# Values of an attention chunk multiplied three chunks behind their scores instead of four, and the normalising chain one chunk sooner

## The chip, the cores and the metric

The kernel runs on one core of one Trainium2 chip. The metric is the device time of one execution in microseconds (us). Three executions of the kernel before took 1441.52, 1445.03 and 1444.88 us, a median of 1444.88 us. Engines go by the profile's names: PE is TensorE (PEld its loading of weights), DVE is VectorE, ACT is ScalarE, POOL is GpSimd, SP is SyncE.

## The reference

The input x is 4 batches of 1024 tokens of width 128. After a layer norm, two branches are added to x: causal attention with 16 heads of width 64, and a mixture of 8 experts of which each token takes two. The change touches the attention alone:

```python
sim = einsum('bhid,bhjd->bhij', q, k)            # q scaled by 64 ** -0.5
attn = softmax(where(causal_mask, -max, sim))
out = einsum('bhij,bhjd->bhid', attn, v)
return out.reshape(b, n, h * d) @ w_out
```

## The kernel before, in words

The first stage (up to about 260 us) does the experts and lays the normalised tokens out. The second stage is the attention, and all of this case lies there. It goes through 64 heads (4 batches x 16 heads), two heads of one batch after each other (a pair shares a projection and half of `w_out`), and eight heads, numbered 0 to 7 here, make a group: one pair of heads over the four batches. Eight groups follow each other.

A head's score matrix is worked off in twelve chunks (`chunks`, L1026), one to each step 0 to 11. A chunk is 128 keys against up to 512 queries; its widths in order are 512, 128, 384, 256 for the first half of the queries, then 512, 128, 512, 256, 512, 384, 512, 512 for the second. The narrower ones lie on the diagonal.

One list, `order`, written out by `beside` (L1064 to L1105), sets the program of every engine: each engine walks through the same list and does its own part of each entry, in order. A step `c` of head `g` enters, in this sequence: the scores of chunk `c` ("score"); the values of the chunk `LAG` steps back ("pv"); one part of the next head's row maxima ("max", in steps 0, 1, 2, 3, 5, 7, 10, 11, L1039); the low part of those values ("pv_low"); in even heads a projection of the next pair ("project", steps 1, 2, 3, 5, 6, 10) with its subtraction ("project_lo"); an output projection ("y", step 11 of even heads and step 10 of odd ones); the transposed maxima ("shift", steps 8 and 0); the entries of `CHAIN`; and a piece of the experts' combination ("gather" in heads 1 and 2, "combine" in heads 3 to 7).

What the entries are on the engines:

- score (L1484): PE multiplies keys by queries (L1497, L1498, and L1500 for a mask). ACT takes the exponential twice (L1281), once to `probs` and once rounded to `p_hi`; POOL subtracts the two to `p_lo` (L1243). There are two score banks, four `probs` and six `p_hi` and `p_lo`.
- pv and pv_low (L1503, L1519): PE multiplies `p_hi` by the values twice (L1514, L1516) and waits for `p_split` before it multiplies `p_lo` (L1525). After the last chunk of a half, ACT copies the sums out to `raw` (L1297), at the place of that "pv_low" in the list.
- max (L1457): PE makes raw scores in `max_ps` (L1472, L1475), and DVE reduces them (`maximum`, L1322, the reduction on L1329). There are two banks; a narrow part takes one and a wide part (the last four) both. PE waits on L1466 until the part named in `BEFORE` (L1043) is reduced; the part of step 5 is wide and so waits for that of step 3.
- project: ACT copies PE's product out (L1259, L1263), DVE subtracts it from the product (L1319, L1307).
- the chain, for each half: SP folds the row sums (L1154), DVE inverts them (L1378), SP stores the inverse to DRAM (L1160) and spreads it back over 64 partitions (L1166), DVE multiplies `raw` by it ("normalise", `heads`, L1384). `LAST` says that a half ends with chunk 3 or 11, and `CHAIN` says how many steps after the scores of that chunk each entry stands.
- combine: DVE's small operations on `x_row` and `gvar` (L1342 to L1372), fed by POOL's gathers of rows (L1236, eight in each group, in steps 7 to 11 of head 1 and 1, 3, 5 of head 2).

The wait between the scores and their low values is this one, with `n_chunk(g, c)` counting chunks:

```python
pe.wait_ge(p_split, n_chunk(g, c) + 1)
pe.matmul(head_ps[0:HEAD + 1, cols], v_hi[i][:, j, s], p_lo[:, slot, 0:width], ...)
```

Of the kernel before, what the change touches and what calls it, by code (L numbers as in the profile page):

```python
# [24 lines left out]
def attention_and_experts(nc, x, attn_gamma, w_qkv, w_out, w_router, b_router,  # L25
# [28 lines left out]
    with ExitStack() as whole:  # L54
# [925 lines left out]
        with ExitStack() as ph2:  # L980
# [48 lines left out]
            CH = len(chunks)  # L1029
            DIAG = [q0 == j * P for _, j, q0 in chunks]  # L1030
            WIDTH = [(half + 1) * BANK - q0 for half, _, q0 in chunks]
            LAG = 4
            CHAIN = [("fold", 5), ("invert", 8), ("store", 9), ("spread", 12), ("normalise", 16)]
            G = BATCH * 2
            ALL_HEADS = PAIRS * G
            ALL_PAIRS = PAIRS * BATCH
# [27 lines left out]
            def beside(at):  # L1064
# [9 lines left out]
                if g == 0 and c in FIRST_WIDE:  # L1074
                    order += [("max", 0, m) for m in FIRST_WIDE[c]]
                values = at >= LAG and (at - LAG) // CH < ALL_HEADS
                if values:
                    order.append(("pv", (at - LAG) // CH, (at - LAG) % CH))
                max_at = MAX_AT if g else FIRST_MAX_AT
                if g + 1 < ALL_HEADS and c in max_at:  # L1080
                    order.append(("max", g + 1, max_at.index(c)))
                if values:
                    order.append(("pv_low", (at - LAG) // CH, (at - LAG) % CH))

# [9 lines left out]
                if g < ALL_HEADS and c == (0 if g else 2):  # L1094
                    order.append(("shift", g, 1))
                for kind, lag in CHAIN:
                    if at >= lag and (at - lag) // CH < ALL_HEADS and (at - lag) % CH in LAST:
# [483 lines left out]
```

## Time and profile before

| | |
|---|---|
| median of three executions | 1444.88 us |
| the profiled execution | 1440.34 us, of which its span is 1438.6 us |
| second stage | from about 260 us to the end |
| PE busy | 1360.5 us, 95% of the span |
| DVE, ACT, POOL busy | 1102.6, 1046.0 and 940.8 us |
| mean granted TensorE clock | 0.983 of full speed |

The span is the time from the first to the last instruction on the core, and the profiled execution's own time is 1.7 us longer than it. Busy shares are averages over the whole span: PE's idle time lies mostly in the first stage, and in the second stage each wait has to be looked up where it stands. A row of a timeline gives the start from the beginning of the span, the length, the engine and line, the operation with its output and inputs, and in brackets how long the engine was idle before and for whom. Several instructions of one kind in a row are merged (x2, x3). Lengths of neighbours overlap somewhat, so that what one costs in a row of its kind is the spacing of their starts.

### The profile page before, as it was taken

How to read it: one execution, taken by the hardware profiler on the slowest of the kernel's cores; microseconds unless marked ns; L12 is line 12 of the kernel's file. 1: busy time of each engine (PE TensorE's matmuls, PEld its weight loads, DVE VectorE, ACT ScalarE, POOL GpSimd, SP SyncE). 2: the span in 40 equal slices, each digit the busy share in tenths (PEclk: the TensorE clock that was granted, in tenths of full speed). 3: DMA queues.
4: the chain of work that ended last, by engine and by line, in shares of the span. 5: the costliest groups of instructions: out<-in, count | busy, mean ns of one | idle time of the engine just before them, and what ended most of it. 6: DMA issues, size and time to landing. Idle time of an engine off the chain costs nothing.

```text
span 1438.6 us, 26847 instructions
## 1 busy us (share of the span) xinstructions
PE 1360.5 (95%) x8618; PEld 1017.9 (71%) x8618; DVE 1102.6 (77%) x1944; ACT 1046.0 (73%) x2571; POOL 940.8 (65%) x933
## 2 busy tenths in 40 slices
PE   2789999899999999999999999999999999999996
PEld 2778999566777676767677767677767676767674
DVE  5756666569877987798869886988698869886974
ACT  1556666587877777778777877787877787778774
POOL 1676000387668766876687668766876687668775
PEclk9789999899999999999999999999999999999998
DMA  9132231121212121212121212121212122212212
GB/s 337 42 102 83 62 92 52 45 64 46 51 46 69 45 52 42 70 43 51 40 71 43 50 40 69 45 51 40 70 44 51 42 67 48 51 46 65 49 46 78
DMA packets 80377, 89.87 MB, mean 62 GB/s; under 512 B 17736, under 2 KB 58992, under 8 KB 80240
## 3 DMA queue, kind: packets, MB, share of 16 engines
q1 hardware_dynamic: 59168, 69.90, 19.2%
q10 hardware_dynamic: 16976, 9.86, 2.2%
q0 software_dynamic: 4096, 8.40, 2.0%
q8 instruction: 72, 1.18, 0.3%
q14 instruction: 65, 0.53, 0.1%
HBM read 37.25 MB, written 16.78 MB: 38 GB/s over the span
## 4 chain that ended last, share of the span: by engine, by line
PE 55%; DVE 21%; POOL 3%; issue 2%; ACT 1%; DMA 1%; POOLq 0%; ACTq 0%
PE max_ps L1472 8%; PE score_ps L1497 7%; PE score_ps L1498 7%; PE head_ps L1525 7%; DVE row_max L1329 7%; PE head_ps L1514 6%; PE head_ps L1516 6%; PE misc_ps L1535 3%; DVE x_row L1342 3%; DVE q_a L1319 3%; PE misc_ps L1453 2%; DVE k_b L1319 2%; POOL p_lo L1243 2%; PE max_ps L1475 2%; DVE heads L1384 2%; PE score_ps L1500 2%
## 5 line engine op out<-in xcount | busy, mean ns | idle before, releaser
L1243 POOL TENSOR_TENSOR p_lo<-probs,p_hi 128x512 fp32r<-128x512 f32 (+3 forms) x768 | 797.2, 1057 | 291.1 <-ACT p_hi L1281 288.1
L1281 ACT ACTIVATE probs<-score_ps 128x512 f32<-128x512 f32 (+3 forms) x768 | 376.7, 491 | 180.9 <-PE score_ps L1500 100.0
L1329 DVE TENSOR_REDUCE row_max<-max_ps 128x1 f32<-128x1024 f32 x508 | 383.5, 756 | 153.0 <-PE max_ps L1475 148.8
L1281 ACT ACTIVATE p_hi<-score_ps 128x512 fp32r<-128x512 f32 (+3 forms) x768 | 376.6, 490 | 0.0
L1497 PE MATMUL score_ps<-q_a,k_a 128*128 128x512 f32 (+3 forms) x768 | 287.2, 374 | 2.4 <-ACTq L1250 1.5
L1525 PE MATMUL head_ps<-p_lo,v_hi 128*65 128x512 f32 (+3 forms) x768 | 276.1, 360 | 1.1 <-POOL p_lo L1243 1.1
L1514 PE MATMUL head_ps<-p_hi,v_hi 128*65 128x512 f32 (+3 forms) x768 | 274.8, 358 | 0.0
L1498 PE MATMUL score_ps<-q_b,k_b 65*128 65x512 f32 (+3 forms) x768 | 267.0, 348 | 0.0
L1516 PE MATMUL head_ps<-p_hi,v_lo 128*64 128x512 f32 (+3 forms) x768 | 258.3, 336 | 0.0
L1472 PE MATMUL max_ps<-k_a,q_a 128*128 128x512 f32 x764 | 230.6, 356 | 19.8 <-DVE row_max L1329 18.9
L1472 PEld LDWEIGHTS max_ps<-k_a,q_a 128*128 128x128 f32 x764 | 130.2, 190 | 71.5 <-DVE row_max L1329 43.5
L1497 PEld LDWEIGHTS score_ps<-q_a,k_a 128*128 128x128 f32 x768 | 146.2, 190 | 37.8 <-ACT p_hi L1281 5.9
L1498 PEld LDWEIGHTS score_ps<-q_b,k_b 65*128 65x128 f32 x768 | 146.2, 190 | 10.0
L1525 PEld LDWEIGHTS head_ps<-p_lo,v_hi 128*65 128x65 f32 x768 | 110.4, 144 | 22.6 <-POOL p_lo L1243 8.4
L1516 PEld LDWEIGHTS head_ps<-p_hi,v_lo 128*64 128x64 f32 x768 | 105.8, 138 | 25.0
L1514 PEld LDWEIGHTS head_ps<-p_hi,v_hi 128*65 128x65 f32 x768 | 111.6, 145 | 11.5
L1384 DVE TENSOR_TENSOR heads<-raw,scale 64x512 f32<-64x512 f32 x128 | 116.3, 909 | 3.0 <-DMA scale<-inv_rows 1.1
L1500 PE MATMUL score_ps<-later,ident 128*128 128x128 bf16 x512 | 118.6, 232 | 0.0
L1475 PE MATMUL max_ps<-ident,later 128*128 128x128 bf16 x508 | 117.3, 231 | 0.0
L1319 DVE TENSOR_TENSOR q_a<-misc_ps,q_a 64x512 fp32r<-64x512 f32 x124 | 85.5, 690 | 36.0 <-ACT q_a L1259 33.2
L1475 PEld LDWEIGHTS max_ps<-ident,later 128*128 128x128 bf16 x508 | 49.0, 96 | 88.5 <-issue 72.8
L553 ACT ACTIVATE w_raw<-bank,b1T 128x128 f32<-128x128 f32 x312 | 88.9, 368 | 24.9 <-PE bank L907 24.3
(190 smaller groups left out, 2171.5 us busy)
## 6 DMA issues: line engine op xcount, KB each, us to landing
k_a<-k_a SPq DMA_DIRECT2D x64, 256.0 KB, 4.0
q_b<-q_a SPq DMA_DIRECT2D x64, 256.0 KB, 4.2
scale<-inv_rows SPq DMA_DIRECT2D x128, 128.0 KB, 2.8
sorted_x<-zeros SPq DMA_DIRECT2D x13, 384.0 KB, 11.6
sorted_y<-result ACTq DMA_DIRECT2D x78, 64.0 KB
w_raw<-sorted_x SPq DMA_DIRECT2D x25, 192.0 KB, 2.4
acc<-in_L_attn_x_dram SPq DMA_DIRECT2D x4, 512.0 KB, 8.1
w_raw<-in_L_ffn_W_dram ACTq DMA_DIRECT2D x4, 512.0 KB, 12.7
```

Of the source, the lines that this page charges most:

```text
L1243: pool.tensor_tensor(p_lo[:, slot, 0:w], probs[:, n_chunk(g, c) % PROBS, 0:w], p_hi[:, slot, 0:w].bitcast(F32), ALU.subtract).then_inc(p_s ...
L1281: ins = act.activation(p[:, n_chunk(g, c) % ring, 0:width], score_ps[n_chunk(g, c) % 2][:, 0:width], ACT.Exp, scale=SCALE)
L1319: ins = dve.tensor_tensor(lo, src[s * HEAD:(s + 1) * HEAD, :], hi, ALU.subtract)
L1329: dve.tensor_reduce(row_max[:, g % 2, t:t + 1], src, axes, ALU.max).then_inc(max_taken, 1)
L1472: ins = pe.matmul(max_ps[:, b, 0:w], rows, k_a[i][s][:, k0:k0 + w], start=True, stop=not last)
L1475: ins = pe.matmul(max_ps[:, b, w - P:w], later[:], ident16[:], start=False, stop=True)
L1497: pe.matmul(dst, k_a[i][s][:, keys], q_a[i][s][:, qs], start=True, stop=False)
L1498: ins = pe.matmul(dst, k_b[i][s][:, keys], q_b[i][s][:, qs], start=False, stop=not DIAG[c])
L1500: ins = pe.matmul(dst[:, 0:P], ident16[:], later[:], start=False, stop=True)
L1514: pe.matmul(head_ps[0:HEAD + 1, cols], v_hi[i][:, j, s], p_hi[:, slot, 0:width], start=(j == 0), stop=False)
L1516: pe.matmul(head_ps[0:HEAD, cols], v_lo[i][:, j, s], p_hi[:, slot, 0:width], start=False, stop=False)
L1525: pe.matmul(head_ps[0:HEAD + 1, cols], v_hi[i][:, j, s], p_lo[:, slot, 0:width], start=False, stop=c in LAST).then_inc(pv_done, 1)
```

## The change

The values follow their scores three steps later instead of four, and each of the five entries of the chain stands one step sooner: the fold 4 steps after the scores instead of 5, the inverse 7 instead of 8, the store 8 instead of 9, the spread 11 instead of 12, the normalising 15 instead of 16. Since the values also come one step sooner, each entry keeps its distance to the values. Banks, rings and every other entry of the list stay where they are.

```diff
-            LAG = 4
-            CHAIN = [("fold", 5), ("invert", 8), ("store", 9), ("spread", 12), ("normalise", 16)]
+            LAG = 3
+            CHAIN = [("fold", 4), ("invert", 7), ("store", 8), ("spread", 11), ("normalise", 15)]
```

In step numbers: the copy to `raw` moves from steps 7 and 3 to 6 and 2, the fold from 8 and 4 to 7 and 3, the inverse from 11 and 7 to 10 and 6, the store from 0 and 8 to 11 and 7, the spread from 3 and 11 to 2 and 10, the normalising from 7 and 3 to 6 and 2 (first half, second half; all of a later head than the scores, except for the first half's copy, fold and inverse).

## Rows read from the trace of the kernel before

**Rows 1.** The page: busy time by engine, share of the span, instructions.
```profile
PE 1360.5 (95%) x8618; PEld 1017.9 (71%) x8618; DVE 1102.6 (77%) x1944; ACT 1046.0 (73%) x2571; POOL 940.8 (65%) x933
```

**Rows 2.** Waits, whole span: who waited for whom, us in total, times, longest us.
```profile
PEld max_ps L1472 <- DVE row_max L1329: 43.5, 85, 1.7
...
PE max_ps L1472 <- DVE row_max L1329: 18.9, 28, 1.4
...
PEld head_ps L1525 <- POOL p_lo L1243: 8.4, 18, 1.2
```

**Rows 3.** Timeline of ACT, steps 2 and 3 of head 0 of group 4.
```profile
708.90 1.21 ACT L1259 ACTIVATE q_a<-misc_ps 64x512 fp32r<-64x512 f32 x2
...
710.68 0.59 ACT L1297 ACTIVATE raw<-head_ps 65x512 f32<-65x512 f32 x1
711.15 1.21 ACT L1259 ACTIVATE k_a<-misc_ps 64x512 fp32r<-64x512 f32 x2
```

**Rows 4.** Timeline of DVE, same head: work entered in steps 2 to 5.
```profile
709.52 1.39 DVE L1319 TENSOR_TENSOR q_a<-misc_ps,q_a 64x512 fp32r<-64x512 f32 x2
710.95 0.69 DVE L1329 TENSOR_REDUCE row_max<-max_ps 128x1 f32<-128x512 f32 x1
711.78 1.39 DVE L1319 TENSOR_TENSOR k_b<-misc_ps,k_a 64x512 fp32r<-64x512 f32 x2
713.09 0.68 DVE L1384 TENSOR_TENSOR heads<-raw,scale 64x512 f32<-64x512 f32 x1
713.79 1.23 DVE L1329 TENSOR_REDUCE row_max<-max_ps 128x1 f32<-128x1024 f32 x1
```

**Rows 5.** Timeline of POOL, same head, step 3.
```profile
710.87 0.74 POOL L1243 TENSOR_TENSOR p_lo<-probs,p_hi 128x256 fp32r<-128x256 f32 x1 [0.84 <-ACT p_hi L1281]
```

**Rows 6.** Timeline of PE, same head: scores of step 4, of step 5, wide maxima.
```profile
710.69 0.40 PE L1497 MATMUL score_ps<-q_a,k_a 128*128 128x512 f32 x1
...
711.87 0.22 PE L1497 MATMUL score_ps<-q_a,k_a 128*128 128x128 f32 x1
...
712.23 0.68 PE L1472 MATMUL max_ps<-k_a,q_a 128*128 128x512 f32 x2
```

**Rows 7.** Timeline of POOL, heads 1 and 2 of group 4: first gather, and after the last.
```profile
734.73 1.24 POOL L1236 DMA_INDIRECT two_y<-sorted_y,places  x1
...
754.52 5.92 POOL L1243 TENSOR_TENSOR p_lo<-probs,p_hi 128x512 fp32r<-128x512 f32 x5
```

**Rows 8.** Timeline of PE, head 2: low values of chunk 5 and of chunk 6.
```profile
753.95 0.22 PE L1525 MATMUL head_ps<-p_lo,v_hi 128*65 128x128 f32 x1
...
755.87 0.47 PE L1525 MATMUL head_ps<-p_lo,v_hi 128*65 128x512 f32 x1
```

**Rows 9.** Timeline of DVE, end of head 2 and start of head 3.
```profile
754.48 1.92 DVE L1384 TENSOR_TENSOR heads<-raw,scale 64x512 f32<-64x512 f32 x1
...
760.70 2.31 DVE L1342 TENSOR_SCALAR x_row<-x_row,mean,rstd 128x128 f32<-128x128 f32 x1
```

**Rows 10.** Timeline of PE: step 7 of head 3, step 11 of head 6.
```profile
768.68 0.68 PE L1472 MATMUL max_ps<-k_a,q_a 128*128 128x448 f32 x2 [0.47 <-DVE row_max L1329]
...
831.80 0.55 PE L1472 MATMUL max_ps<-k_a,q_a 128*128 128x320 f32 x2 [1.38 <-DVE row_max L1329]
```

**Rows 11.** Timeline of DVE, head 4: the chain's operations right behind step 7's maxima.
```profile
791.62 0.33 DVE L1378 RECIPROCAL inv<-den 16x32 f32<-16x32 f32 x1
791.98 0.88 DVE L1384 TENSOR_TENSOR heads<-raw,scale 64x512 f32<-64x512 f32 x1
```

**Rows 12.** Timeline of PE, head 4: maxima of step 7 and of step 10.
```profile
788.48 0.67 PE L1472 MATMUL max_ps<-k_a,q_a 128*128 128x448 f32 x2 [0.22 <-DVE row_max L1329]
...
792.13 0.51 PE L1472 MATMUL max_ps<-k_a,q_a 128*128 128x384 f32 x2
```

**Rows 13.** The chain that ended last, its longest stretch on POOL, last head.
```profile
1409.73 12.61 POOL p_lo L1243 x11
```

**Rows 14.** The page: DMA issues, KB each, us to landing.
```profile
scale<-inv_rows SPq DMA_DIRECT2D x128, 128.0 KB, 2.8
```

## The prediction

> **What bounds the kernel now.** I read the page first: PE is busy for 95% of the span [rows 1], so in the second stage time is gained or lost by what makes PE wait, and by nothing else. The view of waits says for what: PE and its weight loads wait 62 us at most for DVE's row maxima (43.5 and 18.9, partly the same time) and 8.4 us for POOL's low parts, in 18 places [rows 2]. The low values are the wait that the change tightens, since PE asks for them a whole step sooner; the maxima are a wait that it touches indirectly, since it reorders DVE. So I went to the timelines of both, in the heads where little is in hand.
>
> Of 768 low values that is few, and they lie together, once in each group. From head 1's step 7 on, eight gathers of about 1 us stand between POOL's subtractions, and POOL works through from 734.73 to 760.44 [rows 7]. At 755.87 PE starts the low values of chunk 6 the moment POOL delivers them [rows 8]: there even four steps are only just enough. For DVE, head 0 of a group shows what it does in steps 2 to 5 of every even head [rows 4]: after ACT's copy it subtracts a projection (709.52), reduces the maxima of step 3 (710.95), subtracts the next projection, normalises (713.09) and reduces the wide maxima of step 5 (713.79). PE asked for those wide maxima's banks at 712.23 [rows 6]; step 3's were reduced at 711.64, 0.59 before.
>
> **The change part by part.** *Work.* No instruction is added or removed, on any engine. The values run one set ahead of where they were against the scores; over all chunks PE does the same.
>
> *ACT's copy to raw, from step 3 to 2 in even heads.* It now stands ahead of the copies of the projection that DVE waits for. It costs ACT 0.47 (711.15 - 710.68) [rows 3], so those copies start at 709.37 instead of 708.90, and DVE's pair at 709.99 instead of 709.52; the pair takes 1.43 to the next start [rows 4], to 711.42. POOL's subtraction in step 3 moves as much, from 710.87 to 711.34, and ends at 712.08 [rows 5].
>
> *The normalising of the second half, from step 3 to 2.* Before, it stood behind the maxima of step 3 on DVE; now it stands in front of them. That is the edit's dearest effect. Alone it costs 0.70 (713.79 - 713.09) [rows 4]. At 711.42, though, POOL's subtraction has just begun, and both read SBUF. Such meetings are in the trace: the normalising at 754.48, beside a POOL subtraction that starts at 754.52, took 1.92 instead of 0.68 [rows 4, 7, 9]. So it ends at 712.1 at the least and at about 712.7 if it waits, and the maxima of step 3, 0.69 long, are reduced at 712.8 or 713.4. I take the second, because in the nearest row DVE lost even by starting 0.04 sooner.
>
> *What PE asks in step 5.* Step 4 took 1.18 with five 512-wide matmuls, 0.236 each; the five narrow ones before the wide maxima in step 5 took 0.36, 0.07 each [rows 6]. Now step 4's three value matmuls are 128 wide (-0.49) and step 5's first two 384 wide (+0.21): PE asks at 712.23 - 0.28 = 711.95. It waits until 713.4: **1.45 us** per even head (0.87 if normalising does not wait). Behind that wait on PE stand the low values and the third projection of the step, and ACT and DVE wait for the latter. In odd heads there is no projection, DVE idles before these maxima, and I put the same edit at nothing; without that cover it costs up to 0.15 in 24 heads.
>
> *The low values in heads 1 and 2.* POOL's stretch is fixed by its own queue while it is behind. The low values of chunk 6 now stand a step sooner, right where those of chunk 5 stood at 753.95, and POOL is ready at 755.87: 1.92 late. About 0.4 of this the kernel before already pays in the steps around. So 1.5 per group. It falls into the same steps as the 1.45 of head 2 and mostly hides it: I take 1.7, between 1.4 (one hides the other) and 2.9 (both in full).
>
> *Head 3.* DVE's first operation there lasts 2.31, waiting out POOL's backlog [rows 9], and so PE waits in step 7 (0.47 and the weight load before it) [rows 10]. Once PE is late by 1.7 the backlog is gone sooner: 0.6 back, between 0 and 1.1.
>
> *Head 4.* Reciprocal and normalising of the first half move from behind the maxima of step 7 to in front, 1.24 (792.86 - 791.62) [rows 11]. Those maxima were ready at 791.6, and PE asked at 792.13 [rows 12]. DVE is besides 0.6 late (1.4 later, less the 0.7 taken from behind the maxima of step 3): ready at 793.5. PE asks 1.45 later, less 0.5 for the wait of step 7 that falls away (0.22 and its weight load) [rows 12] and 0.23 for narrower values: at 792.85. So it waits 0.65 more, and saves some 0.6 of waits it had: 1.45 + 0.65 - 0.6 = **1.5**. In the other heads I cost it at nothing, because DVE is not late there when it reaches these maxima and PE asks three steps later; without that cover it would be the 0.65 again.
>
> *Head 6.* PE already waits 1.38 for DVE in step 11 [rows 10], so DVE's total decides, which is the same but for the meeting with POOL: 0.6, at least 0.
>
> *SP's queue and the transfers.* Fold, store and spread pass the shift of step 8 or 0 on SP's queue, but their releasers come one step sooner as well. The spread lands in 2.8 us [rows 14] and keeps four steps until the normalising. Nothing, between 0 and 2 us in all.
>
> *The last head.* There POOL is the bound: eleven subtractions, 12.61, without a pause [rows 13]. Its first scores come one set of values later, three matmuls of 384, about 0.5; the values then wait beside POOL and cost nothing.
>
> *Sum.* Head 0: 7 x 1.45 = 10.2 (the very first head has no such step). Heads 1 and 2: 8 x 1.7 = 13.6. Head 3: -8 x 0.6 = -4.8. Head 4: 8 x 1.5 = 12. Head 6: 7 x 0.6 = 4.2 (the last group's has no projection). End: 0.5. Together 35.7: 1440.3 + 35.7 = **1476 us** against the profiled execution, whose median over three executions stands 4.5 higher. I leave it at 1476.
>
> **The rivals.** *Normalising goes first.* If DVE gets through in the even heads, the price is 0.87 in head 0, 1.5 in head 2, 0.8 in head 4 and nothing in head 6: 7 x 0.87 + 8 x 1.5 - 4.8 + 8 x 0.8 + 0.5 = 20, **1460**. It hangs on 0.08 us, the distance of 711.34 and 711.42. The Trainium skill, SBUF — State Buffer, section "Who interferes with whom", says that a DVE instruction with two SBUF inputs contends with a GpSimd one that reads SBUF, and that whichever issues first holds the shared port pair for its whole length; by that rule the sum would be the 20 if DVE issues first and the 35.7 if POOL does. Rows 9 agree that the loser waits.
>
> *POOL alone.* DVE catches up in the gaps before step 5, as it idles in odd heads, and only the backlog after the gathers is left: 8 x 1.5 - 4.8 + 0.5 = 8, **1448**. Against it: in head 0 DVE goes from 709.52 to 713.79 with no pause over 0.2 [rows 4].
>
> *No change.* PE waits 8.4 us for the low parts in 1440 [rows 2]; if DVE's new order is neutral and the backlog is paid back in head 3, the time is **1441**.
>
> *Faster.* Normalising now no longer stands directly ahead of the wide maxima of step 5, and those are what PE waits for in step 7 of heads 3 and 4 (0.47, 0.22) and, through them, in step 11 of head 6 (1.38) [rows 10, 12]. If it slips into an idle stretch of DVE, half of such waits, about 2 us in a group, would go: **1425**. It decides where DVE has at least 0.7 idle ahead of step 3's maxima; head 0 shows none [rows 4].
>
> **How the numbers follow.** Forecast 0.50, normalising first 0.20, POOL alone 0.12, no change 0.11, faster 0.07. About 0.3% (4.3 us) is what a measurement of this kernel can tell from no change. The first three cases are slower by more than that: 0.82. The range starts below the POOL case, at 1446, and ends at the forecast with head 2 at 2.9 (+9.6), odd heads at 0.15 (+3.6) and the median's 4.5 on top: 1494.
>
> **What would show it.** In the profile after: PE waiting for the row maxima in step 5 of even heads, 0.9 to 1.5, which has no such wait now; in the view of waits, PE for DVE's maxima some 20 us up, and PE for POOL's low parts up by about 12, in heads 1 and 2 alone; normalising in step 2 with a length of about 1.2; heads 1, 5 and 7 as long as before. I am wrong if step 3's maxima in even heads are reduced before PE asks, or if the low values of heads 1 and 2 start without waiting.

## The result, and the profile after

Four executions of the changed kernel took 1517.41 to 1530.46 us, a median of **1523.96 us**, beside 1443.56 us for four of the kernel before: a ratio of 1.0557, 95% interval 1.0514 to 1.06. It is slower, as forecast, but by more than twice the 35.7 us of the sum, and 30 us beyond the upper end of the range, 1494. The profiled execution took 1526.43 us, its span 1524.7.

The page's busy times and the view of waits (us in total, times, longest) of the changed kernel, whole span; they answer to [rows 1, 2]:

```profile
PE 1374.8 (90%) x8618; PEld 1029.0 (67%) x8618; DVE 1128.4 (74%) x1944; ACT 1032.8 (68%) x2571; POOL 929.8 (61%) x933
```

```profile
PEld max_ps L1472 <- DVE row_max L1329: 116.0, 120, 4.6
PE max_ps L1472 <- DVE row_max L1329: 81.9, 58, 4.3
...
PEld head_ps L1525 <- POOL p_lo L1243: 14.3, 30, 1.2
PE head_ps L1525 <- POOL p_lo L1243: 8.5, 25, 1.0
```

The last of these lines in the kernel before:

```profile
PE head_ps L1525 <- POOL p_lo L1243: 1.1, 2, 0.7
```

PE does the same work and is idle longer. The change makes the low values more urgent: PE's weight loads wait 14.3 us for them instead of 8.4 [rows 2], PE itself 8.5 instead of 1.1, and the two are partly the same time. The big growth is PE waiting for DVE's maxima, 18.9 to 81.9, with single waits of 4.3 us where 1.4 was the longest.

Where does it lie? The starts of each head's first score matmul (L1497) give the length of all 64 heads. Below are the differences to the kernel before, from the profiled execution of each, summed over the eight groups, beside what the prediction gave.

| us over 8 groups | head 0 | heads 1, 2 | head 3 | head 4 | head 6 | heads 5, 7, start | span |
|---|---|---|---|---|---|---|---|
| predicted | 10.2 | 13.6 | -4.8 | 12 | 4.2 | 0 (end 0.5) | 35.7 |
| measured | 13.1 | **50.5** | -7.2 | 22.3 | 7.3 | 0.1 | 86.1 |

So 37 of the missing 50 lie in head 2 (head 1 is -0.3). The timeline of the changed kernel there, group 4: DVE from step 6 on, POOL beside it, then PE's low values of step 1 and the maxima of step 10 (start, length, and in brackets the idle time ahead):

```profile
787.25 0.33 DVE L1378 RECIPROCAL inv<-den 16x32 f32<-16x32 f32 x1
787.61 4.87 DVE L1384 TENSOR_TENSOR heads<-raw,scale 64x512 f32<-64x512 f32 x1
792.51 1.09 DVE L1329 TENSOR_REDUCE row_max<-max_ps 128x1 f32<-128x896 f32 x1
...
785.56 0.96 POOL L1236 DMA_INDIRECT two_y<-sorted_y,places  x1 [0.16 <-issue]
786.55 5.38 POOL L1243 TENSOR_TENSOR p_lo<-probs,p_hi 128x512 fp32r<-128x512 f32 x5
...
774.47 0.45 PE L1525 MATMUL head_ps<-p_lo,v_hi 128*65 128x512 f32 x1 [0.52 <-POOL p_lo L1243]
...
793.66 0.61 PE L1472 MATMUL max_ps<-k_a,q_a 128*128 128x384 f32 x2 [4.30 <-DVE row_max L1329]
```

The first half's normalising, now in step 6 and so ahead of step 7's maxima, starts while POOL works through its backlog behind the last gather. It needs 0.68 alone [rows 4] and takes 4.87: it ends 0.55 after the whole run of five subtractions, not after the one that it met. Behind it on DVE stand the maxima of step 7, and PE, which asked for their banks at 789.36 (793.66 - 4.30), stands still for 4.30.

It does not end there. Busy time by stretch of the same place (stretch, its length, PE, PEld, DVE, ACT and POOL busy with counts, granted TensorE clock, DMA share, GB/s):

```profile
767.71:793.66 25.95, 20.73 (x125) 14.75 (x124) 18.84 (x23) 18.03 (x42) 22.96 (x23) 1.00 0.35 86
793.66:798.00 4.34, 4.34 (x18) 3.50 (x18) 1.90 (x3) 1.62 (x3) 0.00 (x0) 0.61 0.07 25
798.00:810.00 12.00, 12.00 (x83) 8.83 (x82) 9.24 (x15) 7.78 (x22) 8.44 (x9) 1.00 0.05 13
```

When PE goes on, the granted clock is at its lower level (1.2 GHz) for most of the next 4.34 us: 0.61 on average, an estimated 4.34 x 0.39 = 1.7 us of work lost. Of head 2's 7.1 in this group, 4.3 is this wait, some 1.7 is the clock, and PE's waits for late low values in steps 1 to 3 (0.52, 0.17 and 0.22) make up most of the 1.1 that is left.

The same place in group 5 shows that this is no fixed price. Timeline of the changed kernel, DVE and POOL, head 2 of group 5:

```profile
936.94 2.27 DVE L1384 TENSOR_TENSOR heads<-raw,scale 64x512 f32<-64x512 f32 x1
...
945.99 0.89 DVE L1384 TENSOR_TENSOR heads<-raw,scale 64x512 f32<-64x512 f32 x1
...
937.60 2.19 POOL L1243 TENSOR_TENSOR p_lo<-probs,p_hi 128x384 fp32r<-128x384 f32 x2
...
945.61 0.73 POOL L1243 TENSOR_TENSOR p_lo<-probs,p_hi 128x256 fp32r<-128x256 f32 x1 [0.21 <-ACT p_hi L1281]
```

Here the second half's normalising met POOL at 936.94 and took 2.27, PE waited 1.44 for it in step 5, and POOL caught up: at 945.61 it had a pause ahead, the first half's normalising took 0.89, and PE waited 0.32 in step 10. Head 2 grew by 3.4 and 3.1 in groups 1 and 5 and by 7.1 to 7.9 in the six others. In those six PE does not wait in step 5 of head 2, where the prediction expected it to: the second half's normalising takes 0.68 there in group 4 (at 780.15).

Head 0 went as the prediction worked it out. Timeline of the changed kernel, steps 2 to 5 of head 0 of group 4, answering to [rows 4 to 6]:

```profile
740.94 1.39 DVE L1319 TENSOR_TENSOR q_a<-misc_ps,q_a 64x512 fp32r<-64x512 f32 x2 [0.49 <-ACT q_a L1259]
742.37 1.20 DVE L1384 TENSOR_TENSOR heads<-raw,scale 64x512 f32<-64x512 f32 x1
743.59 0.69 DVE L1329 TENSOR_REDUCE row_max<-max_ps 128x1 f32<-128x512 f32 x1
...
742.29 0.73 POOL L1243 TENSOR_TENSOR p_lo<-probs,p_hi 128x256 fp32r<-128x256 f32 x1 [1.24 <-ACT p_hi L1281]
...
744.34 0.73 PE L1472 MATMUL max_ps<-k_a,q_a 128*128 128x512 f32 x2 [1.19 <-DVE row_max L1329]
```

POOL starts 0.08 before normalising, normalising waits and takes 1.20, the maxima of step 3 follow, and PE loses 1.19 in step 5, where 1.45 was forecast.

And head 4, the second largest miss. Timeline of the changed kernel, steps 6 to 10, group 5, answering to [rows 11, 12]:

```profile
983.05 0.33 DVE L1378 RECIPROCAL inv<-den 16x32 f32<-16x32 f32 x1
983.41 0.90 DVE L1384 TENSOR_TENSOR heads<-raw,scale 64x512 f32<-64x512 f32 x1
984.34 1.26 DVE L1349 SCALAR_TENSOR_TENSOR x_row<-two_y,weights,x_row 128x128 f32<-128x128 f32 x1
985.53 1.08 DVE L1329 TENSOR_REDUCE row_max<-max_ps 128x1 f32<-128x896 f32 x1
...
984.00 3.69 POOL L1243 TENSOR_TENSOR p_lo<-probs,p_hi 128x512 fp32r<-128x512 f32 x3 [0.23 <-ACT p_hi L1281]
...
986.66 0.62 PE L1472 MATMUL max_ps<-k_a,q_a 128*128 128x384 f32 x2 [1.50 <-DVE row_max L1329]
```

The combination's `x_row` behind normalising lost to POOL's subtraction as well (1.26; the same form took 0.43 at 978.60 in this head), and the maxima came 1.50 after PE asked, where the prediction had 0.65.

### The profile page after: what moved, and what is told of

Same layout as the page of the kernel before. It is cut to its first block, busy times and chain, and to the rows that moved or that the text cites. A ratio compares the mean times of both kernels' runs of the same rounds, so it can differ in the third digit from the quotient of the medians.

```text
span 1524.7 us, 26847 instructions
## 1 busy us (share of the span) xinstructions
PE 1374.8 (90%) x8618; PEld 1029.0 (67%) x8618; DVE 1128.4 (74%) x1944; ACT 1032.8 (68%) x2571; POOL 929.8 (61%) x933
## 3 DMA queue, kind: packets, MB, share of 16 engines
q8 instruction: 72, 1.18, 0.3%
## 4 chain that ended last, share of the span: by engine, by line
PE 44%; DVE 14%; POOL 9%; ACT 9%; issue 6%; DMA 0%; POOLq 0%; ACTq 0%
PE max_ps L1472 8%; POOL p_lo L1243 6%; PE head_ps L1525 5%; DVE heads L1384 5%; PE score_ps L1498 5%; PE head_ps L1514 5%; PE score_ps L1497 5%; PE head_ps L1516 5%; DVE row_max L1329 4%; PE misc_ps L1535 3%; POOL two_y L1236 2%; PE misc_ps L1453 2%; DVE q_a L1319 2%; ACT q_a L1259 2%; ACT probs L1281 2%
## 5 line engine op out<-in xcount | busy, mean ns | idle before, releaser
L1243 POOL TENSOR_TENSOR p_lo<-probs,p_hi 128x512 fp32r<-128x512 f32 (+3 forms) x768 | 788.8, 1043 | 385.6 <-ACT p_hi L1281 384.4
L1472 PE MATMUL max_ps<-k_a,q_a 128*128 128x512 f32 x764 | 231.3, 357 | 82.1 <-DVE row_max L1329 81.9
L1497 PE MATMUL score_ps<-q_a,k_a 128*128 128x512 f32 (+3 forms) x768 | 287.5, 374 | 1.7 <-ACTq L1250 1.5
L1472 PEld LDWEIGHTS max_ps<-k_a,q_a 128*128 128x128 f32 x764 | 134.7, 191 | 154.3 <-DVE row_max L1329 116.0
L1497 PEld LDWEIGHTS score_ps<-q_a,k_a 128*128 128x128 f32 x768 | 147.4, 192 | 28.3 <-ACT p_hi L1281 11.7
L1498 PEld LDWEIGHTS score_ps<-q_b,k_b 65*128 65x128 f32 x768 | 147.0, 191 | 15.1
L1384 DVE TENSOR_TENSOR heads<-raw,scale 64x512 f32<-64x512 f32 x128 | 148.3, 1158 | 4.0 <-DMA scale<-inv_rows 1.1
L1525 PEld LDWEIGHTS head_ps<-p_lo,v_hi 128*65 128x65 f32 x768 | 111.0, 144 | 20.8 <-POOL p_lo L1243 14.3
```

Source lines behind the costliest of these rows:

```text
L1243: pool.tensor_tensor(p_lo[:, slot, 0:w], probs[:, n_chunk(g, c) % PROBS, 0:w], p_hi[:, slot, 0:w].bitcast(F32), ALU.subtract).then_inc(p_s ...
L1384: dve.tensor_tensor(heads[s * HEAD:(s + 1) * HEAD, cols], raw[0:HEAD, s, half], scale[:, half], ALU.mult).then_inc(normalised, 1)
L1472: ins = pe.matmul(max_ps[:, b, 0:w], rows, k_a[i][s][:, k0:k0 + w], start=True, stop=not last)
L1497: pe.matmul(dst, k_a[i][s][:, keys], q_a[i][s][:, qs], start=True, stop=False)
L1498: ins = pe.matmul(dst, k_b[i][s][:, keys], q_b[i][s][:, qs], start=False, stop=not DIAG[c])
```

## The experiments

Thirteen kernels, none of which leaves work out. A time is that of one execution, except for e7, e9 and e13, which are medians of several and have intervals. The table gives the same per-head differences to the kernel before for each; "1st/2nd" is the distance of normalising for the first and second half in steps.

| run | values | 1st/2nd | other | us | head 0 | head 2 | head 3 | head 4 | head 6 |
|---|---|---|---|---|---|---|---|---|---|
| changed | 3 | 15/15 | | 1523.96 | 13.1 | 50.8 | -7.2 | 22.3 | 7.3 |
| e1 | 3 | 16/16 | | 1481.43 | 1.4 | 31.6 | 0.3 | 3.5 | 3.9 |
| e2 | 4 | 15/15 | | 1447.84 | 4.4 | 0.6 | -3.3 | 14.1 | -8.2 |
| e3 | 3 | 15/15 | gathers spread | 1485.04 | 13.1 | 10.3 | -7.2 | 22.4 | 7.3 |
| e4 | 3 | 16/15 | | 1496.71 | 9.9 | 28.0 | -1.6 | 9.3 | 9.9 |
| e5 | 3 | 15/15 | 1st at 14 in head 2 | 1486.01 | 12.7 | 9.9 | -7.3 | 22.4 | 7.3 |
| e6 | 3 | 15/15 | raw a step later | 1475.25 | 8.3 | 12.4 | -7.2 | 17.8 | 3.8 |
| e7 | 4 | 16/16 | gathers spread | 1432.45 | 0.2 | -5.2 | -5.7 | 0.0 | 0.0 |
| e8 | 3 | 16/16 | gathers spread | 1490.25 | 23.2 | 20.4 | -2.0 | 3.5 | 3.9 |
| e9 | 4 | 16/16 | gathers spread, 1st at 15 in head 6 | 1431.02 | -0.3 | -5.2 | -5.7 | -0.1 | -1.2 |
| e10 | 3 | 15/16 | 1st at 14 in head 2 | 1475.58 | 3.7 | 12.4 | -7.4 | 27.3 | 1.1 |
| e11 | 5 | 17/17 | gathers spread | 1575.11 | 33.9 | 33.6 | -3.2 | 35.4 | 24.7 |
| e12 | 3 | 14/16 | | 1463.48 | 3.1 | 12.1 | -7.3 | 15.2 | 0.1 |
| e13 | 3 | 14/16 | gathers spread | 1450.52 | 2.6 | -0.9 | -7.4 | 15.1 | 0.0 |

**e1 and e2: one half of the change each.** e1 keeps the values at three and puts normalising back:

```diff
-            CHAIN = [("fold", 4), ("invert", 7), ("store", 8), ("spread", 11), ("normalise", 15)]
+            CHAIN = [("fold", 4), ("invert", 7), ("store", 8), ("spread", 11), ("normalise", 16)]
```

> The changed kernel with one entry put back: normalising 16 steps after the scores instead of 15 (steps 7 and 3 again); values three steps back, raw, fold, inverse, store and spread as changed. Theory A (the cost is DVE's order: normalising stands in front of the row maxima of steps 3 and 7): nearly all of the 82 us is gone; what stays is the shorter lead of the low values behind the gathers, about 1.5 us in each of 8 groups, less what head 3 gives back: 1445 to 1458 us, no PE wait for the maxima in step 5 of heads 0, 4 and 6, normalising in head 2 under 2.5 us. Rival B (the cost is that PE asks for the low values a step sooner): normalising's place is of no account, 1505 to 1530 us.

e2 is the kernel before with normalising alone one step sooner:

```diff
-            CHAIN = [("fold", 5), ("invert", 8), ("store", 9), ("spread", 12), ("normalise", 16)]
+            CHAIN = [("fold", 5), ("invert", 8), ("store", 9), ("spread", 12), ("normalise", 15)]
```

> The kernel before with one entry changed: normalising 15 steps after the scores instead of 16; values four steps back and everything else as before. Theory A: most of the loss is there although no low value is asked for sooner: the second half's normalising meets POOL's subtraction (about 1.2 us) in front of step 3's maxima, so PE waits 0.5 to 0.9 us in step 5 of heads 0, 4 and 6, and the first half's waits out POOL's backlog in head 2 for 3 to 5 us: 1475 to 1510 us. Rival B: 1441 to 1447 us, as before.

Measured: 1481.43 and 1447.84 (1444.51 for the kernel before beside them). Theory A, that the order on DVE is the whole loss, missed in both. Rival B missed in e1 (1505 to 1530) and came within 1 us of e2 (1441 to 1447). The new order alone costs 3 us, less than executions of the kernel before differ by (1439.11 to 1448.32); the values alone 37; both together 80. The two work on each other. e1 shows how: head 2 still loses 31.6 with normalising behind the maxima of step 7. Its timeline, DVE, POOL and PE in head 2 of group 4:

```profile
771.40 4.36 DVE L1384 TENSOR_TENSOR heads<-raw,scale 64x512 f32<-64x512 f32 x1
775.79 0.96 DVE L1329 TENSOR_REDUCE row_max<-max_ps 128x1 f32<-128x768 f32 x1
...
769.79 5.41 POOL L1243 TENSOR_TENSOR p_lo<-probs,p_hi 128x512 fp32r<-128x512 f32 x5
...
776.80 0.41 PE L1472 MATMUL max_ps<-k_a,q_a 128*128 128x320 f32 x1 [2.06 <-DVE row_max L1329]
```

The same long normalising, one set of maxima later in the list: now those of step 10 are late, and PE waits in step 11.

**e3, e4 and e5: what starves head 2.** e3 takes POOL's backlog away by spreading the eight gathers over heads 0 to 2 of the changed kernel:

```diff
-            GATHER_AT = [(1, c) for c in (6, 7, 8, 9, 10, 11)] + [(2, c) for c in (1, 3, 5)]
+            GATHER_AT = [(0, c) for c in (0, 3, 7, 11)] + [(1, c) for c in (3, 7, 11)] + [(2, c) for c in (3, 7)]
```

> The changed kernel with POOL's eight gathers of a group spread over heads 0 to 2 (steps 3, 7, 11, then 3, 7, 11, then 3, 7) instead of heads 1 and 2 (every step from 7 on, then 1, 3, 5). Theory A says that the 51 us of head 2 come from POOL's backlog of five subtractions, which normalising waits out with PE waiting for the maxima behind it: without the backlog head 2 is as heads 0 and 6 (about 22 us instead of 27.6), 40 to 50 us less in all, 1475 to 1490 us, and normalising nowhere over 1.5 us. Rival C (DVE starves beside POOL whenever head 2 comes, with or without the gathers): 1510 us or more.

Measured: 1485.04. Head 2 falls from 50.8 to 10.3 and every other head stays within 0.2: its loss comes from POOL's backlog.

e4 puts the first half's normalising back to 16 in all heads and leaves the second half's at 15:

```diff
-                for kind, lag in CHAIN:
+                for kind, lag in CHAIN + [("normalise", 16)]:
+                    if kind == "normalise" and (at - lag) % CH != LAST[16 - lag]:
+                        continue
```

> The changed kernel with the first half's normalising alone put back, from step 6 to step 7 behind the maxima; the second half's stays in step 2. Theory A: head 2's long wait in step 10 (4.3 us) and those of heads 4 and 6 in step 10 (1.4 us each) go, the waits of step 5 (1.2 us in heads 0, 4, 6) stay: 1460 to 1485 us. Rival D (the second half's place in front of step 3's maxima makes DVE late for all that follows, step 10 included): 1505 us or more.

Measured: 1496.71, between what theories A and D expected. Head 2 keeps 28.0, much as in e1: behind the maxima of step 7 normalising still lies inside the backlog, and takes 3.96 (at 778.96, group 4).

e5 moves the first half's normalising in head 2 alone, one step sooner, to step 5, where POOL is in gathers:

```diff
-                for kind, lag in CHAIN:
+                for kind, lag in CHAIN + [("normalise", 14)]:
+                    if kind == "normalise" and (lag == 14) != (
+                            (at - lag) % CH == LAST[0] and ((at - lag) // CH + 1) % G == 2):
+                        continue
```

> The changed kernel with one instruction in each group moved: the first half's normalising in head 2 enters at step 5 instead of step 6, so that it starts while POOL issues a gather or pauses instead of 1.06 us into a subtraction with four more behind it. Theory E (a DVE operation with two SBUF inputs that starts inside a POOL subtraction waits until POOL pauses, one that starts ahead of it waits for one at most): it takes under 2.3 us instead of 4.87, PE's 4.3 us wait in step 10 of head 2 shrinks to under 1, and 8 x 3 to 4 us go: 1490 to 1502 us, heads 0, 4 and 6 unchanged. Rival F (DVE is late there by the sum of its work, the long normalising only shows it): the wait moves to the next maxima, 1515 us or more.

Measured: 1486.01, less than the 1490 to 1502 that theory E gave. One instruction per group moved by one step gives 38 us back against the median. Timeline of e5 (its lines stand 3 lower), DVE and POOL, head 2 of group 5:

```profile
923.40 0.69 DVE L1387 TENSOR_TENSOR heads<-raw,scale 64x512 f32<-64x512 f32 x1
...
923.52 1.41 POOL L1239 DMA_INDIRECT two_y<-sorted_y,places  x1 [0.16 <-issue]
924.95 5.43 POOL L1246 TENSOR_TENSOR p_lo<-probs,p_hi 128x512 fp32r<-128x512 f32 x5
```

Normalising falls beside the gather and takes 0.69; the gather, 0.97 elsewhere in this head, took 1.41. The run of five subtractions still follows, and nothing on DVE is held up beside it.

**e6: the copy to `raw`.** The prediction charged ACT's copy 0.47 ahead of the projection's copies. e6 puts it back to four steps behind the scores:

```diff
+                if at >= LAG + 1 and (at - LAG - 1) // CH < ALL_HEADS and (at - LAG - 1) % CH in LAST:
+                    order.append(("raw", (at - LAG - 1) // CH, (at - LAG - 1) % CH))
...
-                        elif kind == "pv_low" and c in LAST:
+                        elif kind == "raw":
```

> The changed kernel with ACT's copy to raw alone put back to where it stood, four steps after the scores of its chunk (steps 7 and 3), behind the exponentials of that step; the fold then waits for it in the same step. Step of the prediction: raw ahead of the projection's copy makes DVE's pair and step 3's maxima 0.47 us late. If that holds, PE's wait in step 5 of heads 0, 4 and 6 goes from 1.19 to about 0.7 and these heads get 0.4 to 0.6 shorter: 9 to 13 us from 22 heads, 1505 to 1517 us where head 2 stays as it is. Rival: ACT catches up, the waits stay at 1.1 to 1.2, 1517 to 1530 us. Head 2 may go either way by up to 4 us in each group, as its normalising starts 0.5 us sooner against POOL.

Measured: 1475.25, below the 1505 to 1517 expected. PE's wait in step 5 of heads 0, 4 and 6 of group 5 falls from 1.18, 1.17 and 1.11 to 0.79, 0.79 and 0.77, so the copy is worth 0.34 to 0.39 there, somewhat less than its 0.47. The larger part of the gain is head 2, 38 less: DVE comes by at another moment there and the long normalising does not occur. That was not what the edit was for.

**e7 and e8: the gathers spread without the change, and with the order put back.** e7 is the kernel before, e8 is e1, each with e3's line of gathers.

> The kernel before (values four steps back) with the gathers spread over heads 0 to 2 as in the run with spread gathers. Theory: POOL's backlog costs the kernel before about 0.6 us in head 2 and 1.0 in head 3 of each group; without it both go: 1428 to 1436 us. Rival: DVE's waits in head 3 are its own work, only 0.6 x 8 go: 1438 to 1442 us.

> Values three steps back, normalising 16 steps after the scores, gathers spread. If values three steps back cost only through the backlog behind the gathers (late low values, and normalising that starts inside a subtraction), head 2 is as short as head 0 (about 20 us, not 24.5) and all is 1436 to 1450 us. Rival B (the shorter lead itself costs): 1465 us or more, with PE waiting for POOL's low parts outside heads 1 and 2.

Measured: e7 1432.45 (four executions, 1429.57 to 1433.73), ratio 0.9911, interval 0.9895 to 0.9928: **faster than both kernels**, by 0.9%, as expected: by 5.2 in head 2 and 5.7 in head 3, where PE waited behind the backlog. e8 missed its expectation widely: 1490.25, and head 0, which lost 1.4 in e1, lost 23.2. Rival B's time (1465 or more) fits, its reason does not: PE itself waits 1.0 us in all for low values. Timeline of e8, DVE and POOL, head 0 of group 4, with the last subtraction of the run by itself:

```profile
738.73 4.57 DVE L1384 TENSOR_TENSOR heads<-raw,scale 64x512 f32<-64x512 f32 x1
...
738.28 0.97 POOL L1236 DMA_INDIRECT two_y<-sorted_y,places  x1
739.26 5.16 POOL L1243 TENSOR_TENSOR p_lo<-probs,p_hi 128x512 fp32r<-128x512 f32 x4
...
742.71 1.72 POOL L1243 TENSOR_TENSOR p_lo<-probs,p_hi 128x512 fp32r<-128x512 f32 x1
```

One gather, put at step 7 of head 0, is enough to make POOL run four subtractions without a pause. Normalising started ahead of all four, came in behind the third and took 4.57; the fourth, 1.72 long where the third took 1.27, then waited for it. So no large backlog is needed, only that POOL goes straight on while DVE wants in. Theory E of e5, by which an operation that starts ahead of a subtraction waits for one at most, falls here. PE waits 2.4 in step 11 of heads 0 and 2.

**e9, e10 and e11: two attempts at better, and the opposite direction.** e9 is e7 with the first half's normalising at 15 in head 6 alone:

```diff
-                for kind, lag in CHAIN:
+                for kind, lag in CHAIN + [("normalise", 15)]:
+                    if kind == "normalise" and (lag == 15) != (
+                            (at - lag) % CH == LAST[0] and ((at - lag) // CH + 1) % G == 6):
+                        continue
```

> The kernel before with the gathers spread (as in the run that gave 1432.45), and in head 6 alone the first half's normalising 15 steps behind its scores instead of 16, so that it stands in step 6, ahead of step 7's maxima. Theory H (head 6 waits in step 11 only because normalising stands directly ahead of the wide maxima that PE wants there): the wait of some 1.4 in step 11 of head 6 goes, as in the run where all first halves were normalised in step 6 (head 6 was 8.2 shorter over the eight groups), and the other heads stay: 1421 to 1427. Rival K (the starts of normalising against POOL's subtractions decide, and any shift of 1 us in head 6 moves those of the heads behind it): head 6 gains its 8, but heads 0 and 2 of the next group change by as much either way: 1428 to 1440.

Measured: 1431.02 (four executions), ratio 0.9905, interval 0.9888 to 0.9921. Neither theory was right: nothing else moved, but head 6 gains only 1.2 in all. PE's 1.38 in step 11 became 1.11 in step 10. The wait was not removed, it was moved.

e10 undoes two parts of the change at once:

```diff
-                for kind, lag in CHAIN:
+                for kind, lag in CHAIN + [("normalise", 14), ("normalise", 16)]:
+                    if kind == "normalise":
+                        done, half = (at - lag) // CH, (at - lag) % CH
+                        if lag != (16 if half == LAST[1] else 14 if (done + 1) % G == 2 else 15):
+                            continue
```

> The changed kernel with two parts undone at once: the second half's normalising back at 16 steps (behind the maxima of step 3), the first half's at 14 in head 2 (ahead of the stretch in which POOL works without a pause) and at 15 in the others. Theory E (the loss is the sum of two places, step 5 of even heads and step 10 of head 2): head 2's 4.3 in step 10 is gone and so are the waits of 1.1 in step 5; left are the low values of head 2 (1.2 to 2 per group), head 4's wait in step 10 and the end: 1450 to 1465, head 0 within 3 us of before over all groups. Rival K (phase decides): normalising meets a run of POOL's subtractions somewhere else, in a wait of 2 or more in step 10 or 11 of head 2 or head 0: 1470 to 1490.

Measured: 1475.58, in rival K's range, but not for its reason: no normalising took over 1.7. Theory E's two places are mended as expected (head 0 at 3.7, no wait of 1.1 in step 5, nothing above 0.35 in steps 9 to 11 of head 2), but 27.3 stays in head 4, where PE waits 1.63 in step 10. Theory E had named that wait, but its 1450 to 1465 left far too little for it. PE's maxima of step 10 there, and the stretches of e10 ahead of that wait's end and behind it, head 4 of group 5:

```profile
956.18 0.62 PE L1476 MATMUL max_ps<-k_a,q_a 128*128 128x384 f32 x2 [1.63 <-DVE row_max L1333]
...
954.50:957.00 2.50, 0.87 (x6) 0.66 (x6) 2.22 (x5) 0.94 (x2) 2.50 (x3) 0.97 0.44 89
957.00:960.00 3.00, 3.00 (x13) 2.50 (x12) 1.48 (x3) 0.98 (x2) 0.21 (x1) 0.50 0.00 0
```

Here too the clock falls to 0.50 behind the wait, for 3 us: an estimated 1.5 lost besides the 1.63.

e11 goes the other way, to values five behind, with e3's line of gathers:

```diff
-            LAG = 4
-            CHAIN = [("fold", 5), ("invert", 8), ("store", 9), ("spread", 12), ("normalise", 16)]
+            LAG = 5
+            CHAIN = [("fold", 6), ("invert", 9), ("store", 10), ("spread", 13), ("normalise", 17)]
```

> The other direction: values five chunks behind their scores, the chain one step later than before (fold 6, inverse 9, store 10, spread 13, normalising 17), gathers spread. Theory L (an order of the list is good where normalising stands behind all maxima that PE wants soon): normalising stands in step 8 and step 4. In step 4 it is directly ahead of the wide maxima of step 5, where before it stood in step 3 behind those of step 3, so nothing new is ahead of a part that PE asks for; the low values have a step more: within 8 us of 1432, thus 1424 to 1440. Rival K (phase decides): some head has normalising waiting out four or more of POOL's subtractions: 1445 to 1475, with such a length of 4 us or more in the rows of L1384.

Measured: 1575.11, worse than the change and for a reason of which neither theory spoke. Timeline of e11, SP's queue and DVE, head 0 of group 5, and the view of waits of DVE (kernel before: 4.6 us in 2 places):

```profile
926.63 0.49 SPq L1175 DMA_DIRECT2D k_a<-k_a  x1
...
928.45 1.19 SPq L1176 DMA_DIRECT2D q_b<-q_a  x1
929.68 1.21 SPq L1154 DMA_DIRECT2D den<-raw  x1
...
934.17 0.34 DVE L1378 RECIPROCAL inv<-den 16x32 f32<-16x32 f32 x1 [4.24 <-DMA den<-raw]
```

```profile
DVE inv L1378 <- DMA den<-raw: 109.7, 31, 5.0
```

The fold of the second half, entered in step 5, now stands on SP's queue behind the four copies of a pair's projections, which wait for ACT until 926.6; the sums had been ready since 924.9. DVE goes on 4.5 after its issue, having stood 4.24 at the inverse, and PE stands 3.84 at the maxima of step 11. No normalising took over 1.8 in this run. The cause is read from this timeline: no run moved the fold alone.

**e12 and e13: head 4, and all places mended.** The changed kernel with the second half at 16 and the first at 14 in every head; e13 spreads the gathers besides:

```diff
-            CHAIN = [("fold", 4), ("invert", 7), ("store", 8), ("spread", 11), ("normalise", 15)]
+            CHAIN = [("fold", 4), ("invert", 7), ("store", 8), ("spread", 11), ("normalise", 14)]
...
-                for kind, lag in CHAIN:
+                for kind, lag in CHAIN + [("normalise", 16)]:
+                    if kind == "normalise":
+                        if lag != (16 if (at - lag) % CH == LAST[1] else 14):
+                            continue
```

> The changed kernel with the second half's normalising back at 16 steps, and the first half's at 14 in every head: it stands in step 5, behind that step's maxima, instead of directly ahead of those of step 7. Theory M (head 4 pays because normalising stands directly ahead of step 7's maxima, which PE waits for in step 10): head 4's sum falls from the 27.3 of the run with 15 to below 8 and its wait in step 10 from 1.6 to under 0.3; head 2 stays at about 12 (the low values alone): 1452 to 1462. Rival N (DVE is simply late in head 4, by the combination's operations, whatever the order): head 4 stays above 20: 1468 to 1480.

> The same, with the gathers spread over heads 0 to 2 as well, so that POOL has no backlog in head 2. Theory M: head 2's 12 goes too and the 5 of head 3 come back as in the run of the kernel before with spread gathers: 1432 to 1445, no better than that run, because values three steps behind give PE nothing that it waited for. Rival K (phase decides): a normalising waits out four or more of POOL's subtractions in head 0 or 2, and PE waits 2 or more behind it: 1455 to 1490.

Measured: 1463.48, and 1450.52 for e13 (five executions), ratio 1.0034, interval 1.0019 to 1.0048. Head 4 keeps 15.2 and 15.1, between what theories M and N gave. Timeline of e13 (lines 3 lower), DVE and PE, head 4 of group 5:

```profile
939.41 1.18 DVE L1387 TENSOR_TENSOR heads<-raw,scale 64x512 f32<-64x512 f32 x1
...
941.49 0.73 DVE L1352 SCALAR_TENSOR_TENSOR x_row<-two_y,weights,x_row 128x128 f32<-128x128 f32 x1
942.15 1.08 DVE L1332 TENSOR_REDUCE row_max<-max_ps 128x1 f32<-128x896 f32 x1
...
943.28 0.62 PE L1475 MATMUL max_ps<-k_a,q_a 128*128 128x384 f32 x2 [1.46 <-DVE row_max L1332]
```

A step sooner, normalising meets another subtraction (1.18) and PE's wait is 1.46, 0.17 shorter than e10's. So the place directly ahead of step 7's maxima is not what costs: theory M falls. Ahead of them at all costs 1.5 a group; only behind them is it nearly free (e1, which differs from e12 in this entry alone: 3.5 in head 4 for 15.2), so N's "whatever the order" falls too. The 12 us between e10 and e12 in head 4 are the clock: in e12 the same stretch behind the wait, of 1.48, stands at full clock:

```profile
953.00:956.00 3.00, 3.00 (x24) 2.59 (x23) 2.25 (x5) 1.58 (x3) 0.63 (x2) 1.00 0.11 32
```

Between e12 and e13 head 2 goes from 12.1 to -0.9, and PE's wait for low values from 12.1 to 1.2 us in the whole span: the **late low values cost some 12 to 13**, and spread gathers take that away. Even so e13 missed theory M's 1432 to 1445, by head 4.

## Why the prediction was wrong in its size

**The direction and its reason held.** PE's wait for DVE's maxima is what grew, by 63.0 where some 20 was forecast. In head 0 each link came as forecast: the copy to `raw` delays the projection (e6), POOL gets in first by 0.08, normalising takes 1.20, PE waits in step 5. Of the 1.94 measured per group, 1.36 remain when only the second half's normalising is early (e4), against 1.45 predicted, and about 0.57 when only the first half's is (e12, at 14), which the prediction had at nothing. So "normalising goes first" is refuted for head 0; heads 1, 5 and 7 are as long as before, within 0.3 each.

**The step that failed is the term of heads 1 and 2, 1.7 a group**, through something put at nothing. The term priced the late low values (1.5 a group, 12 in all; e12 shows 12.1) and step 5. What it left out is the sentence under head 4 that moves the first half's normalising: "In the other heads I cost it at nothing". Head 2 is one of those, and there this normalising moves into POOL's backlog, takes 4.87 and keeps PE waiting 4.30. e5 puts a size on that: 50.8 less 9.9 is 41 of the 50 us that the sum lacked, the clock that falls behind the long wait included, which no term of the sum had. Besides, the price of a meeting, half a microsecond, was that of one subtraction. The rows already showed more: 2.31 for `x_row` [rows 9], which the prediction read as waiting out a backlog but carried over to no other place. And the run behind the last gather is twice as long as it was read: [rows 7] shows five subtractions, to 760.44, because the window asked for ended at 760. POOL in a longer window of the kernel before:

```profile
754.52 10.49 POOL L1243 TENSOR_TENSOR p_lo<-probs,p_hi 128x512 fp32r<-128x512 f32 x10
```

It runs ten subtractions without a pause, to 765.01, and `x_row` at 760.70 waited for two of them.

**Head 4 was mis-sized**, 1.5 predicted and 2.8 measured. Its parts: PE waits 1.17 in step 5, for the 1.45 of the sum, and the first half's normalising ahead of step 7's maxima costs some 1.5 a group (e12 against e1), where the prediction had 0.65 less 0.6 saved. It counted normalising and the inverse, but not that the combination's `x_row` behind them then meets POOL (1.26 for 0.43), nor that DVE's only pause ahead of step 7's maxima, 0.87 before 982.44, lies before them.

**Head 6 and head 3** went the right way (7.3 for 4.2, -7.2 for -4.8). **The transfers** cost nothing, as predicted: DVE waits 1.1 us for the spread in both kernels. e11 shows that this was not a general freedom: one step the other way, DVE waits 109.7 us for the fold on the same queue. **The last head** changed by -0.15 where 0.5 was put.

**The rivals.** "POOL alone", 1448, has its mechanism and its 12 us right, but even with DVE's order mended as far as e12 does the time is 1463.48, because head 4 stays. "No change" and "faster" are refuted; what "faster" hoped for is seen only with values four behind, where PE's wait in step 11 of head 6 goes (e2, head 6 8.2 shorter). What was missing among them is one in which a normalising loses to a whole run of POOL's subtractions in head 2: 4.3 of wait in six groups of eight is 26 us more, and 36 with 1.7 of clock each.

**Open.** Whether normalising gets between two of POOL's subtractions (2.27 at 936.94, 0.89 at 945.99) or waits out the run (4.87, 4.36) or most of it (4.57) depends on the moment at which it comes. Edits elsewhere (e6, e8) turned it on or off. At the same moment it comes out the same: in six groups of the changed kernel normalising started 1.06 to 1.09 into a subtraction and lasted 4.84 to 4.87. But the length of the run does not decide: in the kernel before, normalising at 754.48 stood ahead of ten subtractions and came in behind the first [rows 9]. Of 128 normalisings in each run, 6, 8, 8 and 15 took over 3 us in the changed kernel, e1, e4 and e8 (5.91 at the most, in e8), and none in the others. Which moment decides, no run settled.

## What to carry to other kernels

An operation moved up on an engine is priced in every place in which it recurs, not in the one where it was studied: list what stands beside it and behind it in each head, above all where another engine for which it was seen to wait runs without a pause. Before asking for a result sooner, spread what makes its producer late: here the gathers, without any change of the values, gave 0.9%. Ask for a window of the timeline that ends behind the run that you read: a run cut off by the window's end looks like a short one. And on a queue that runs in order, a shift by one step is free only until the entry passes behind one that waits.

## What the runs showed of the hardware that was not expected

A DVE operation with two inputs in SBUF can wait far longer than one operation of POOL: 64x512 elements, 0.68 alone, took 4.87, 4.36, 3.96 and 4.57 (changed kernel, e1, e4, e8) beside runs of four or five subtractions with no pause between them. The Trainium skill, SBUF — State Buffer, section "Who interferes with whom", says that whichever issues first holds the shared pair for its whole instruction. The rows agree that the loser is blocked (1.20 at 742.37, behind one subtraction); by the rule taken alone, normalising at 787.61 would have had its turn when the subtraction then running ended, and it had it only after the fifth. The measurement decides: the holder's next instructions can come first.

The granted clock fell behind waits of 4.30 (changed kernel: 0.61 over the next 4.34 us) and 1.63 (e10: 0.50 over 3 us), and stayed at 1.00 behind one of 1.48 (e12). The length of the wait alone does not decide. Stretches of e8 behind two waits of 2.43, in head 2 of group 1 and head 0 of group 4:

```profile
326.12:330.12 4.00, 4.00 (x17) 3.18 (x18) 2.18 (x4) 0.28 (x1) 0.07 (x1) 0.57 0.09 26
744.34:748.34 4.00, 4.00 (x29) 3.17 (x30) 2.48 (x5) 1.54 (x5) 1.54 (x3) 1.00 0.09 25
```

PE had stood still as long in both, and the granted clock is 0.57 behind the one and 1.00 behind the other. The kernel before had no wait of PE for the maxima above 1.4 [rows 2], and its granted clock stood at 1.00 from 290 to 1410 us, so a forecast that only adds up waits came out too low.

The opposite of the long normalising happens as well: a gather on POOL took 1.41 in place of 0.97 where DVE's normalising had started 0.12 ahead of it (e5, at 923.52). Where the gather had started first, by 0.28, both took their usual time (changed kernel, at 780.15: 0.68 and 0.96). And a change of the gathers that gives 11 us in one schedule (e7, span) cost 9 in another (e8 against e1), where normalising met an unbroken run of POOL's in head 0 as well.
